# A quantised FFN on one core: a signed maximum in pass 1, and the act magnitudes moved to the scalar engine

## The reference

```python
def act_qdq(x):                       # qmax = 32767
    scale = jnp.maximum(jnp.max(jnp.abs(x)) / qmax, 1e-12)
    return jnp.clip(jnp.round(x / scale), -qmax - 1.0, qmax) * scale
...
x = act_qdq(x)
up = act_qdq(x @ lpbq_dequant(w_up).T)
gate = act_qdq(x @ lpbq_dequant(w_gate).T)
sig = fixed_qdq_u16(jax.nn.sigmoid(gate))
gate = act_qdq(gate * sig)
o = act_qdq(gate * up)
return o @ lpbq_dequant(w_down).T
```

## Time and profile before

| | us |
|---|---|
| median of three runs (lowest, highest) | 990.96 (990.79, 992.87) |
| the profiled execution | 992.62 |
| span in its trace | 990.8 |
| PE busy | 901.8 (91%) |
| DVE busy | 654.7 (66%) |
| ACT busy | 445.9 (45%) |

### The profile page before, as it was taken

How to read it: one execution, slowest core, us unless ns; L and a number is a source line. 1 busy time by engine, 2 the same in 40 slices (tenths; PEclk the granted TensorE clock), 3 DMA queues, 4 the chain that set the end, 5 groups by cost and what they waited for, 6 DMA issues and landing times.

```text
span 990.8 us, 13547 instructions
## 1 busy us (share of the span) xinstructions
PE 901.8 (91%) x4904; PEld 487.8 (49%) x4904; DVE 654.7 (66%) x755; ACT 445.9 (45%) x469; POOL 4.0 (0%) x17
## 2 busy tenths in 40 slices
PE   6999998999999999999999999990029999999998
PEld 5999994444444444444444444440014444444443
DVE  0365778756656654469788789758987787876511
ACT  1112341433333333398787782228875444544000
POOL 0000000000000000000000000000000000000000
PEclk9999998999999999999999999995559999999999
DMA  8998864323352222579999635999987799988221
GB/s 282 376 385 298 292 217 173 125 98 127 127 222 96 97 95 95 218 268 419 374 380 388 241 127 195 390 423 362 417 333 268 275 348 344 345 304 319 85 85 64
DMA packets 67768, 249.67 MB, mean 252 GB/s; under 512 B 5971, under 2 KB 5971, under 8 KB 67731
## 3 DMA queue, kind: packets, MB, share of 16 engines
q1 hardware_dynamic: 58354, 198.72, 54.5%
q10 hardware_dynamic: 9376, 50.48, 12.6%
HBM read 175.51 MB, written 73.66 MB: 251 GB/s over the span
## 4 chain that ended last, share of the span: by engine, by line
PE 86%; DMA 5%; DVE 4%; ACT 2%; issue 2%; DVEq 0%; POOL 0%; SPq 0%; ACTq 0%; POOLq 0%
PE bank L705 16%; PE bank L706 16%; PE bank L707 16%; PE bank L655 11%; PE bank L740 6%; PE bank L741 6%; PE bank L742 6%; DMA up_ring<-up_scratch 3%; ACT umag L607 2%; PE wt_bank L666 2%; PE bank L643 1%; DMA x_ring<-in_x_dram 1%; PE bias_bank L741 1%; PE wt_bank L740 1%; PE wt_bank L741 1%
## 5 line engine op out<-in xcount | busy, mean ns | idle before, releaser
L527 ACT ACTIVATE stage<-bank 128x512 f32<-128x512 f32 x192 | 112.9, 593 | 228.6 <-PE bank L707 218.0
L934 DVE TENSOR_REDUCE tile_max<-stage 128x1 f32<-128x1536 f32 (+1 forms) x62 | 108.4, 1749 | 41.9 <-ACT stage L527 41.9
L740 PE MATMUL bank<-wt_down,o_even 128*128 128x512 f16 x192 | 73.8, 384 | 66.7 <-DVE o_even L1142 66.7
L705 PE MATMUL bank<-xq_head,wt_gate 128*128 (+1 forms) x336 | 128.3, 382 | 4.3 <-DVE xq_head L921 4.3
L706 PE MATMUL bank<-xq_head,wt_gate 128*128 (+1 forms) x336 | 128.4, 382 | 0.0
L707 PE MATMUL bank<-xq_head,wt_gate 128*128 (+1 forms) x336 | 128.2, 382 | 0.0
L705 PE MATMUL bank<-xq_head,wt_up 128*128 x336 | 127.3, 379 | 0.0
L706 PE MATMUL bank<-xq_head,wt_up 128*128 x336 | 127.3, 379 | 0.0
L707 PE MATMUL bank<-xq_head,wt_up 128*128 x336 | 127.3, 379 | 0.0
L655 PE MATMUL bank<-xt,w_ring 128*128 128x128 f32 x1024 | 121.6, 278 | 2.2 <-ACT xt L480 2.2
L655 PEld LDWEIGHTS bank<-xt,w_ring 128*128 128x128 f32 x1024 | 118.9, 195 | 2.4 <-ACT xt L480 2.4
(11 more groups left out here) (156 smaller groups left out, 1361.6 us busy)
## 6 DMA issues: line engine op xcount, KB each, us to landing
up_ring<-up_scratch SPq DMA_DIRECT2D x60, 768.0 KB, 7.0
w_ring<-in_L_cond_W_dram SPq DMA_DIRECT2D x32, 1024.0 KB, 7.2
gate_scratch<-stage ACTq DMA_DIRECT2D x32, 768.0 KB, 3.3
gate_ring<-gate_scratch SPq DMA_DIRECT2D x32, 768.0 KB, 7.9
up_scratch<-stage ACTq DMA_DIRECT2D x32, 768.0 KB, 7.0
product_scratch<-prod_ring SPq DMA_DIRECT2D x19, 768.0 KB, 6.4
back_ring<-product_scratch SPq DMA_DIRECT2D x19, 768.0 KB, 13.1
gate_even<-gate_scratch SPq DMA_DIRECT2D x16, 768.0 KB, 7.4
```

The lines of the kernel that those rows point to most:

```text
L527: nc.scalar.activation(stage[:, q % 2, n % PIECE_TILES, :], psum[n % BANKS][:, :], ACT.Copy)\
L705: nc.tensor.matmul(bank[:, :], w_hi, x_hi, start=(k == 0), stop=False)
L740: nc.tensor.matmul(bank, o_hi, wt_down[:, 0, k, :], start=(k == 0), stop=False)
L934: V.tensor_reduce(tile_max[:, side, bass.ds(Q * i + q, 1)], stage[:, q % 2, :, :].rearrange("p t c -> p (t c)"), AX.X, ALU.max, apply_abso ...
```

## The change

Pass 1. The product is now of the signed code and `sigq`, multiplied by -1 inside the same instruction, so its running maximum is that of the negative side. The positive side comes from the largest gate of each partition and piece: in the gate projection, each `piece_max` with side 0 (and `last_piece_max(0)`, in its two parts) has a second reduce ahead of the one it had, a plain maximum of the same staged data into `gate_top`. After piece 0 of pass 1, ACT makes 33 codes and sigmoids from `gate_top` (`top_codes`), and DVE their products (`top_products`). All magnitudes `cmag` are gone, ACT's and DVE's. `code` has three buffers where it had two, `sigq` two where it had one.

Pass 2. ACT makes the act codes (`act_code`, ACT.Abs with the scale, since the products are signed), one after most of the copies in chunks 5 to 7; DVE makes none.

The schedule. Pass 1 has 6, 6, 6, 7, 7 pieces in chunks 0 to 4, where it had 6, 5, 6, 5, 6 and 4 in chunk 5. The 19 pieces stored and the 13 kept are others: kept are 8, 14, 20, 22, 26 (in `prod_kept`), 23, 24, 25, 27 and the last four.

```diff
-PASS1 = (6, 5, 6, 5, 6, 6, 0, 0)
+PASS1 = (6, 6, 6, 7, 7, 0, 0, 0)
+IN_RING, IN_KEPT = (23, 24, 25, 27), (8, 14, 20, 22, 26)
+KEPT_CHUNKS = (1, 2, 3, 3, 4)
-PASS2 = {5: (0, 0, 3, 4), 6: (4, 4, 4, 4), 7: (4, 4, 1, 0)}
+PASS2 = {5: (0,) + (1,) * 11, 6: (1, 1, 1, 1, 1, 2, 1, 1, 1, 1, 1, 1), 7: (1,) * 8 + (0,) * 4}
...
+            def top_codes():
+                nc.scalar.activation(top_code[:, :], gate_top[:, :], ACT.Copy, scale=k_g).then_inc(top_coded, 1)
+                act.wait_ge(top_coded, 1)
+                nc.scalar.activation(top_sig[:, :], top_code[:, :], ACT.Sigmoid, scale=s_g).then_inc(top_sig_made, 1)
...
             def gate_code(j):
...
-                if j >= 2:
-                    act.wait_ge(sig_made, j - 1)
-                    act.wait_ge(mag_scalar if mag_by_act(j - 2) else mag_vector, mags_to(j - 2))
+                if j >= 3:
+                    act.wait_ge(sig_made, j - 2)
+                    act.wait_ge(product_made, j - 2)
...
+            def act_code(m):
+                act.wait_ge(scale_ready, R_ACT)
...
+                    act.wait_ge(back_in[back_slot(k)], 16 * (k // AHEAD) + 16)
...
+                nc.scalar.activation(act_piece(n), src, ACT.Abs, scale=k_p).then_inc(act_made, 1)
...
             def piece_max(i, q, side):
                 dve.wait_ge(tile_copied, NT * (CHUNKS * side + i) + PIECE_TILES * (q + 1))
+                whole = stage[:, q % 2, :, :].rearrange("p t c -> p (t c)")
+                if side == 0:
+                    V.tensor_reduce(gate_top[:, bass.ds(Q * i + q, 1)], whole, AX.X, ALU.max)
+                V.tensor_reduce(tile_max[:, side, bass.ds(Q * i + q, 1)], whole, AX.X, ALU.max,
+                                apply_absolute_value=True).then_inc(piece_maxed, 1)
...
-                V.tensor_scalar(cmag[:, j % 2, :], code[:, j % 2, :], -1.0, None, ALU.mult).then_inc(neg_made, 1)
-                dve.wait_ge(neg_made, mags_to(j))
-                V.tensor_tensor(cmag[:, j % 2, :], code[:, j % 2, :], cmag[:, j % 2, :], ALU.max).then_inc(mag_vector, 1)
...
-                V.tensor_tensor_reduce(product_at(j), cmag[:, j % 2, :], sigq[:, :], 1.0, 0.0, ALU.mult, ALU.max,
-                                       p_max[:, j:j + 1]).then_inc(product_made, 1)
+                V.tensor_tensor_reduce(product_at(j), code[:, j % 3, :], sigq[:, j % 2, :], -1.0, 0.0, ALU.mult, ALU.max,
+                                       p_max[:, TOPS + j:TOPS + j + 1]).then_inc(product_made, 1)
```

More of the change, by code:

```diff
@@ L28 @@
 BANKS = 6
-PASS1 = (6, 5, 6, 5, 6, 6, 0, 0)
+PASS1 = (6, 6, 6, 7, 7, 0, 0, 0)
 LEAD = 8
 RING = 4
-SPILLED = 19
-KEPT = PIECES - SPILLED
+IN_RING, IN_KEPT = (23, 24, 25, 27), (8, 14, 20, 22, 26)
+KEPT_CHUNKS = (1, 2, 3, 3, 4)
+KEPT_ORDER = IN_RING + IN_KEPT + tuple(range(PIECES - RING, PIECES))
+SPILLED_ORDER = tuple(j for j in range(PIECES) if j not in KEPT_ORDER)
+RING_ORDER = SPILLED_ORDER + IN_RING
+SPILLED, KEPT = len(SPILLED_ORDER), len(KEPT_ORDER)
 AHEAD = 6
-PASS2 = {5: (0, 0, 3, 4), 6: (4, 4, 4, 4), 7: (4, 4, 1, 0)}
+PASS2 = {5: (0,) + (1,) * 11, 6: (1, 1, 1, 1, 1, 2, 1, 1, 1, 1, 1, 1), 7: (1,) * 8 + (0,) * 4}
 MSLOTS = 4
-ACT_MAG = 3
 ACT_QMAX = 32767.0
@@ L77, in adaln_ffn @@
         wd_tile = place("wd_tile", 88 * K, [INNER], f32)
-        code = place("code", 80 * K, [2, PIECE], i16)
-        sigq = place("sigq", 86 * K, [PIECE], u16)
-        cmag = place("cmag", 89 * K, [2, PIECE], i16)
+        code = place("code", 80 * K, [3, PIECE], i16)
+        sigq = place("sigq", 89 * K, [2, PIECE], u16)
         act_codes = place("act_codes", 0, [PIECES, PIECE], i16)
@@ L156, in product_at @@
                 return gate_ring[:, j % RING, :]
-            return prod_ring[:, j % RING, :] if j < SPILLED + RING else prod_kept[:, j - SPILLED - RING, :]
+            if j in IN_KEPT:
+                return prod_kept[:, IN_KEPT.index(j), :]
+            return prod_ring[:, RING_ORDER.index(j) % RING, :]
         def back_slot(k):
@@ L187, in stored @@
             return 16 * (PIECES // 2 * side + Q // 2 * (n // Q) + n % Q // 2 + 1)
[L189 to L195, removed]
         def due(count, at, of):
@@ L374, in _ @@
                 load_gate(j + RING)
[L375 removed]
+                if j - 1 in SPILLED_ORDER:
                     store_product(j - 1)
@@ L562, in gate_code @@
                 act.wait_ge(gate_in[j % RING], 16 * (j // RING) + 16)
-                if j >= 2:
-                    act.wait_ge(sig_made, j - 1)
-                    act.wait_ge(mag_scalar if mag_by_act(j - 2) else mag_vector, mags_to(j - 2))
-                nc.scalar.activation(code[:, j % 2, :], gate_ring[:, j % RING, :], ACT.Copy, scale=k_g)\
+                if j >= 3:
+                    act.wait_ge(sig_made, j - 2)
+                    act.wait_ge(product_made, j - 2)
+                nc.scalar.activation(code[:, j % 3, :], gate_ring[:, j % RING, :], ACT.Copy, scale=k_g)\
                     .then_inc(code_made, 1)
@@ L572, in sigmoid @@
                     act.wait_ge(sigq_made, j - 1)
-                nc.scalar.activation(sig[:, j % 2, :], code[:, j % 2, :], ACT.Sigmoid, scale=s_g)\
+                nc.scalar.activation(sig[:, j % 2, :], code[:, j % 3, :], ACT.Sigmoid, scale=s_g)\
                     .then_inc(sig_made, 1)
[L576 to L582, removed]
+            def act_code(m):
+                act.wait_ge(scale_ready, R_ACT)
+                if m < KEPT:
+                    j = KEPT_ORDER[m]
+                    src = product_at(j)
+                else:
+                    k = m - KEPT
+                    j = SPILLED_ORDER[k]
+                    act.wait_ge(back_in[back_slot(k)], 16 * (k // AHEAD) + 16)
+                    src = back_ring[:, back_slot(k), :]
+                n = gate_piece(j)
+                used = -(-(3 * (n + 1) - 24) // 8)
+                if used > 0 and 3 * n < 80:
+                    act.wait_ge(tile_done, NT * (CHUNKS + min(used, CHUNKS - 1)))
+                if m >= RING:
+                    act.wait_ge(act_made, m - 2)
+                nc.scalar.activation(act_piece(n), src, ACT.Abs, scale=k_p).then_inc(act_made, 1)
+            j = m = 0
             for c in range(CHUNKS):
@@ L591, in _ @@
                         sigmoid(j)
-                        if mag_by_act(j):
-                            code_magnitude(j)
+                        if j == 0:
+                            top_codes()
                         j += 1
-            assert j == PIECES
+                    for _ in range(PASS2[c][n] if c in PASS2 else 0):
+                        act_code(m)
+                        m += 1
+            assert j == m == PIECES
             def up_magnitude(k):
@@ L940, in last_piece_max @@
                     dve.wait_ge(tile_copied, NT * CHUNKS * (side + 1) - PIECE_TILES + b)
-                    V.tensor_reduce(tile_max[:, side, PIECES - 1 + n:PIECES + n],
-                                    stage[:, 1, a:b, :].rearrange("p t c -> p (t c)"),
+                    part = stage[:, 1, a:b, :].rearrange("p t c -> p (t c)")
+                    if side == 0:
+                        V.tensor_reduce(gate_top[:, PIECES - 1 + n:PIECES + n], part, AX.X, ALU.max)
+                    V.tensor_reduce(tile_max[:, side, PIECES - 1 + n:PIECES + n], part,
                                     AX.X, ALU.max, apply_absolute_value=True)\
@@ L1040, in max_step @@
[L1040 to L1045, removed]
+                V.tensor_scalar(sigq[:, j % 2, :], sig[:, j % 2, :], 65536.0, 65535.0, ALU.mult, ALU.min)\
                     .then_inc(sigq_made, 1)
-                if j + 1 < PIECES and not mag_by_act(j + 1):
-                    code_magnitude(j + 1)
-                dve.wait_ge(mag_scalar if mag_by_act(j) else mag_vector, mags_to(j))
+                dve.wait_ge(code_made, j + 1)
@@ L1059, in act_step @@
[L1059 to L1073, removed]
@@ L1077, in _, with top_products @@
+            def top_products():
+                dve.wait_ge(top_sig_made, 1)
+                V.tensor_scalar(top_sigq[:, :], top_sig[:, :], 65536.0, 65535.0, ALU.mult, ALU.min)\
+                    .then_inc(top_sigq_made, 1)
+                dve.wait_ge(top_sigq_made, 1)
+                V.tensor_tensor(p_max[:, 0:TOPS], top_code[:, :], top_sigq[:, :], ALU.mult).then_inc(top_product_made, 1)
+            j = 0
+            waiting = False
             for c in range(CHUNKS):
                 for n in range(NT):
-                    q = n // PIECE_TILES
@@ L1080, in _ @@
                     if n % PIECE_TILES == PIECE_TILES - 1:
[L1081 to L1084, removed]
+                        if c == CHUNKS - 1 and n == NT - 1:
                             last_piece_max(1)
                         else:
-                            piece_max(c, q, 1)
+                            piece_max(c, n // PIECE_TILES, 1)
```

48 lines of the change are left out of this document (28 added, 20 removed).

## The result

The changed kernel takes 1002.0 us (median of four runs, 1000.18 to 1002.56), the kernel before 991.58 us beside it (990.79 to 992.87). The ratio is 1.0095, 95% interval 1.0078 to 1.0112. The profiled execution took 1001.58 us with a span of 999.8, 9.0 more than before in both.

A forecast was written before the change was run, and what follows sets the result against it. PE, busy 901.8 of 990.8 us, was taken to bound the kernel; gate-projection delays of 5.0 + 1.5 + 0.6 + 0.6 = 7.7 us on 990.96 gave 998.7 us, range 995.0 to 1003.0.

The forecast's parts named there:

- A plain reduce costs what an absolute one does: Gate projection on DVE: each added plain maximum of 128 x 1536 takes 1.67 us, like the absolute one.
- Rival 3: Plain reduce is fast, 0.87 us; only three ordinary gate boundaries cost, 2.6 us in all, 993.6 us; chance 0.05.
- Three boundaries, 5.0 us: Entering gate chunks 1, 2 and 3, the last piece's extra reduce delays the low part: 3 x 1.67 = 5.0 us.
- rival 4: Gate boundaries: something other than DVE's low part holds the transposes, so reduces hide; no change, 991.0 us; chance 0.06.
- Late chunk 0, 1.5 us: Gate projection, late chunk 0: extra reduces delay two low parts on DVE, making PE 1.52 us late in all.
- Late chunk 4, 0.6 us: Gate projection, late chunk 4: second low part lets PE go at 320.3, against transposes at 319.74; 0.6 us.
- entering chunks 5 and 6, 0.6 us: Gate projection: slack of 1.38 us against an extra 1.67 costs 0.29 at each of two entries, 0.6 us.
- From gate to up, pass 1, pass 2: nothing: Gate-to-up transition and up projection: later gate scale and work shifted between DVE and ACT stay hidden from PE; 0 us.
- Rival 1: Up projection stalls: ACT holds bank copies back while waiting for loaded pieces; PE loses about 3 us, 1001.7; chance 0.10.
- The matmul-free stretch: nothing: Between up and down projection: the pace stays that of the loads and DVE's 32 maxima; 0 us.
- Rival 5: Product maxima in the stretch without matmuls run back to back, 2.8 us gained; 988.2 us; chance 0.05.
- rival 2: Clock falls after new idle stretches at all three gate boundaries, 3 x 2.3 = 7 us more, 1005.7 us; chance 0.06.

The follow-up runs named there:

- the kernel with the reordering: Changed kernel with gate-projection piece maxima on DVE moved behind low parts, at boundaries and in late chunks; 988.25 us, ratio 0.9964 to the kernel before.
- the double: Changed kernel with one more plain reduce of each chunk's last gate piece, its result unread; ratio 1.0237 to the kernel before.

## Why the prediction was right, point by point

The forecast was 998.7 us, in a range of 995.0 to 1003.0; the time is 1002.0, slower as said.

- *A plain reduce costs what an absolute one does*, 1.67 us from start to start. Right: 1.67 (228.90 to 230.57). Rival 3 is out. The Trainium skill's single speed for `tensor_reduce` (VectorE: DVE Perf Modes, the perf-mode tier table) agrees with these rows.
- *Three boundaries, 5.0 us.* Right: 1.67 + 1.66 + 1.66. This also puts out rival 4, since the kernel with the reordering has no wait there.
- *Late chunk 0, 1.5 us.* Right: 1.42, with two waits of 0.92 and 0.77 us. The first was to be 0.54; PE came there earlier, its clock having risen sooner at the start.
- *Late chunk 4, 0.6 us, and entering chunks 5 and 6, 0.6 us.* 0.34, and 0.30 + 0.29. The first was too large by a quarter of a microsecond. PE's waits came to 9.1 us in six places where 9.9 in about nine were forecast.
- *From gate to up, pass 1, pass 2: nothing.* Right, by PE's 248.40 busy us of 248.40, and by the kernel without the reduces, at 0.9998. The 245.7 us of the prediction were misread: in the kernel before the first up matmul starts at 420.5 us, not at 423, and the stage has the same 248.4 us. ACT's wait for the act scale was 1.2 us, not 2.5. The last act code was made at 671.3 us, 8.3 ahead of the start of the last copy of an up tile, which is the distance forecast (661 against 669.3). Rival 1 had the right place to look at (ACT is busy for 198 of 248 us) and nothing happened there.
- *The matmul-free stretch: nothing.* Right within what profiles spread. Rival 5 is out.
- *The clock.* This is where the sum was short. I had it as rival 2, all three boundaries at 2.3 us each, with a chance of 0.06, because the one idle stretch of nearly the same length in the kernel before had kept the clock. It is neither none nor all: five of nine such waits brought it down, at 1.5 to 1.7 us each here. The mean of that is near 2.7 us for three boundaries, and with the 7.3 us of the waits it makes 10.0, close to the 10.4 us between the medians. The error was to take one row at 2.2 us as an answer, and to weigh the event as a case of its own where it was a term of the sum with a bound of 0 and 7 us. That row didn't even answer for itself: behind the same stretch the clock was low in six of ten profiles. The Trainium skill (TensorE: Matmul & The Clock Gate, Part 1) says that the same kernel shows a different number of slow matmuls at its start from run to run. The profiles here show such chance inside the kernel as well, with low clocks behind the third boundary in one execution and behind the first two in another.

So the mechanism and its place were right, the terms of the waits came to 7.3 us for 7.7, and the one low-clock stretch of 1.7 us brought the profiled execution to 1001.58 us where 1000.3 had been forecast. Of the 3.3 us by which the median lies above the forecast, 0.6 are the median before, now 991.58 for 990.96. The narrower range, 996.5 to 1000.5, was missed. That the wide one held was in part luck: its upper end of 1003.0 was argued from stalls of the up projection (rival 1), of which there were none, and from longer register work, of which no run shows any. It left room for the clock that the sum had at nothing.

## What to carry to other kernels

An engine that is 66% busy can have no slack at all at one place of every loop turn; the small wait (here 0.8 us, three times) is the sign of it, and a new instruction there costs its full 1.67 us from start to start while the same one elsewhere is free. The sign isn't complete: 2.3 of the 7.3 us were lost in late chunk 0 and in chunks 4 to 6, where PE had not waited before but had less slack than the new instructions take. So ask of an added instruction not how busy its engine is, but which instruction behind it another engine waits for, and put the work that can come later behind that one. It wasn't free of waits here (19.1 us of ACT's copies), but PE, with six banks, did not wait. Where the new wait leaves PE idle for over two microseconds, add the price of a lower clock to the sum as a term with bounds.

## What the runs showed that I had not expected

PE's granted clock fell behind none of three idle stretches of 1.5 to 1.6 us, nor behind two of 1.8 us in the double, behind five of nine of 2.3 to 2.4 us, and behind all thirteen of 4.0 to 4.3 us. The 2.2 us stretch in the category matmuls, which kept it in the profile before, is in every profile, and behind it the clock fell in six of ten. The same program differed in this from execution to execution. In some cases the clock was low already when the transposes began (0.50 in the first window), in others it fell about 1 us after them. Each cost 1.3 to 2.6 us of slower matmuls on top of the wait.
